# Layers 1 and 2 of a four-layer kernel: narrow products with exchanged operands, and the two token halves woven together

## The reference

```python
# layer 1: attention with the context as keys and values, then low-rank experts
a = jnp.einsum('bqd,bkd->bqk', query, key); c = softmax(a) @ key
q = x @ Wq_w.T; scores = q @ keys.T                  # 64 experts
top_vals, top_idx = jax.lax.top_k(scores, 16); gate = one_hot(top_idx) * softmax(top_vals), summed
z = x @ A_w.T                                        # 64 experts x rank 8
out = (z * gate) @ B_w.T * 2
# layer 2: attention, then three dense experts (tanh, gelu, silu), two of them chosen by sequence
Q = text @ Wq.T + bq; K = features @ Wk.T + bk; attended = softmax(Q @ K.T / sqrt(512)) @ features
gate_logits = concat([h, modality_ratio]) @ gate_w + gate_b
```

## Time and profile before

| what | before |
|---|---|
| median of 3 runs | 1708.53 us (1702.16 to 1709.68) |
| the profiled execution, its time | 1711.2 us |
| its span, first to last instruction | 1709.4 us |
| mean granted clock of TensorE | 0.893 |
| PE busy | 1443.9 us (84%) |
| PEld busy | 1131.2 us (66%) |
| DVE busy | 1083.9 us (63%) |
| ACT, POOL busy | 458.6 us (27%), 296.5 us (17%) |
| DMA, mean over the span | 56 GB/s |

### The profile page before, as it was taken

How to read it: one execution, slowest core, us unless ns; L and a number is a source line. 1 busy time by engine, 2 the same in 40 slices (tenths; PEclk the granted TensorE clock), 3 DMA queues, 4 the chain that set the end, 5 groups by cost and what they waited for, 6 DMA issues and landing times.

```text
span 1709.4 us, 18898 instructions
## 1 busy us (share of the span) xinstructions
PE 1443.9 (84%) x6489; PEld 1131.2 (66%) x6489; DVE 1083.9 (63%) x2489; ACT 458.6 (27%) x994; POOL 296.5 (17%) x170
## 2 busy tenths in 40 slices
PE   6569999998999898899646878858999778789998
PEld 5347776776677667688545767747887546567786
DVE  4556876767777666948886756554446399944142
ACT  3223423332343333313131202101221333322010
POOL 4101111111111111202021002111543121012120
PEclk9779999999999999999855699557999889899999
DMA  5521232322232212222001112200112000001011
GB/s 184 159 77 46 80 82 68 82 74 58 64 89 71 75 50 69 72 66 67 25 26 46 42 40 60 63 18 1 50 49 62 26 25 1 1 27 60 16 36 49
DMA packets 99407, 96.40 MB, mean 56 GB/s; under 512 B 13138, under 2 KB 72418, under 8 KB 99314
## 3 DMA queue, kind: packets, MB, share of 16 engines
q1 hardware_dynamic: 98802, 94.35, 19.0%
q0 software_dynamic: 512, 0.85, 0.2%
HBM read 84.34 MB, written 10.82 MB: 56 GB/s over the span
## 4 chain that ended last, share of the span: by engine, by line
PE 62%; DVE 25%; issue 4%; ACT 4%; DMA 2%; SPq 1%; POOL 1%; DVEq 0%; ACTq 0%; POOLq 0%
PE bank L1636 48%; PE bank L1977 5%; PE bank L1728 4%; DVE nf_y L1581 3%; DVE st L1141 2%; DVE xn L1159 1%; PE bank L1661 1%; DVE xT L1118 1%; PE bank L1718 1%; DVE mx L1192 1%; DVE mx L1498 1%; ACT e L936 1%; DMA nf_w<-in_L_w 1%; DVE sm L1510 1%; SPq L767 1%
## 5 line engine op out<-in xcount | busy, mean ns | idle before, releaser
L1636 PE MATMUL bank<-xT,slots 128*128 128x512 f32 (+1 forms) x1920 | 467.6, 402 | 9.6 <-DVE xT L1118 7.8
L1636 PEld LDWEIGHTS bank<-xT,slots 128*128 128x128 f32 (+1 forms) x1920 | 354.8, 186 | 109.0 <-issue 8.9
L813 POOL TENSOR_TENSOR slots<-staging,slots 128x1024 fp32r<-128x1024 f32 (+4 forms) x97 | 230.5, 2379 | 1103.0 <-ACT slots L903 1103.0
L1581 DVE TENSOR_SCALAR nf_y<-nf_w 128x512 fp32r<-128x512 f32 (+2 forms) x495 | 232.2, 496 | 29.0 <-PE bank L1977 28.0
L1636 PE MATMUL bank<-slots,h 128*128 128x512 f32 (+1 forms) x728 | 178.8, 405 | 20.1 <-DVE h L1248 13.9
L1977 PE MATMUL bank<-nf_y,nf_d 128*128 128x512 f32 (+2 forms) x495 | 170.6, 429 | 10.3 <-DVE nf_y L1581 8.0
L1636 PEld LDWEIGHTS bank<-slots,h 128*128 128x128 f32 (+1 forms) x728 | 140.8, 194 | 56.1 <-DVE h L1248 14.8
L903 ACT ACTIVATE slots<-staging 128x1024 fp32r<-128x1024 f32 (+4 forms) x97 | 98.1, 1018 | 189.9 <-PE bank L1636 174.2
L936 ACT ACTIVATE e<-bank,mx 128x320 f32<-128x320 f32 x128 | 66.4, 523 | 271.1 <-DVE mx L1195 254.0
L1977 PEld LDWEIGHTS bank<-nf_y,nf_d 128*128 128x128 f32 (+1 forms) x495 | 95.3, 197 | 47.0 <-issue 15.5
L1214 DVE TENSOR_TENSOR x<-bank,x 128x512 f32<-128x512 f32 x72 | 49.7, 690 | 110.9 <-PE bank L1636 110.6
(11 more groups left out here) (246 smaller groups left out, 1897.8 us busy)
## 6 DMA issues: line engine op xcount, KB each, us to landing
staging<-in_L_wqkT SPq DMA_DIRECT2D x16, 480.0 KB, 3.8
nf_out<-nf_w SPq DMA_DIRECT2D x30, 256.0 KB, 2.1
staging<-nf_out SPq DMA_DIRECT2D x30, 256.0 KB, 2.8
staging<-in_L_woT SPq DMA_DIRECT2D x16, 384.0 KB, 3.5
staging<-in_L_w SPq DMA_DIRECT2D x12, 512.0 KB, 4.0
nf_a<-nf_max SPq DMA_DIRECT2D x40, 128.0 KB, 3.6
nf_r<-nf_rcp SPq DMA_DIRECT2D x40, 128.0 KB, 3.4
nf_w<-in_L_w SPq DMA_DIRECT2D x15, 256.0 KB, 4.4
```

Of the source, the lines that this page charges most:

```text
L813: g.tensor_tensor(lo, split_source(i), hi.bitcast(FP32), ALU.subtract).then_inc(*sig.mark("weight_low", i))
L1581: v.tensor_scalar(nf_y[0:rows, i % STAIR_RING, 0:size], w_, bound, first, compare, ALU.mult)\
L1636: ins = mm(dst, l_, r_, start=i == 0, stop=i == len(passes) - 1)
```

## The change

*Operands exchanged.* `raw1(layer, b)` makes the scores transposed: 64 key columns are stationary and 256 token columns move, 12 passes a sequence. ScalarE copies them to `raw` (in layer 2 with the scale and, as a bias, `c2T`), and `scores1` is now two PE transposes back to 128 tokens by 64. `raw_route1(half)` and `raw_gate2(half)` do the same with 64 and 4 stationary columns and 512 moving ones, ScalarE copies to `rawT`, and four transposes a half bring them back. Routing then runs on four tiles at once (`route1(half)`, `gates1(half)`). The probabilities stay unscaled; the scale goes into the add to `x`. `pv1` is parted into `probs1` (transposes, splits) and `pv1`. `c2` has 4 stationary columns in place of 128 and is transposed by `c2t`.

*Halves woven.* `schedule` puts `k2` and `m2` between the products of attention 1, routing and `z1(0)` of half 0 before the end of half 1's attention, `stats(3,1)` before the first `zt1`, and the scores of half 0 of layer 2 before the last `b1`. The background ends before `raw_gate2(0)`. Weight chunks `k2` and `m2` are loaded before `z1` and `b1`; the gate weights, `wq1` and `keyT` are loaded in layer 0, where `router1` runs as well. `h2` is parted into four tensors, one of them above the background's memory.

```diff
-BACKGROUND_END = "gate2"
+BACKGROUND_END = "raw_gate2"
@@ schedule @@
-    steps += [("down0", 0, t) for t in range(TILES)]
+    steps += [("down0", 0, t) for t in range(TILES)] + [("router1",)]
...
+    steps += [("k2", 0), ("raw1", 1, 0), ("raw1", 1, 1), ("k2", 1), ("scores1", 1, 0), ("bias2",), ("k2", 2),
+              ("scores1", 1, 1), ("turn", 2, 1), ("probs1", 1, 0), ("k2", 3), ("raw1", 1, 2), ("pv1", 1, 0),
+              ("probs1", 1, 1), ("raw1", 1, 3), ("c2",), ("scores1", 1, 2), ("pv1", 1, 1), ("stats", 3, 0),
+              ("m2", 0), ("probs1", 1, 2), ("scores1", 1, 3), ("m2", 1), ("pv1", 1, 2), ("m2", 2), ("turn", 3, 0),
+              ("raw_route1", 0), ("probs1", 1, 3), ("z1", 0), ("c2t",), ("route1", 0), ("pv1", 1, 3), ("m2", 3),
+              ("gates1", 0), ("stats", 3, 1)]
...
+    after = {0: [("turn", 3, 1), ("raw_route1", 1)], 1: [("route1", 1)], 2: [("gates1", 1)],
+             4: [("stats", 4, 0)], 6: [("turn", 4, 0), ("raw1", 2, 0), ("raw1", 2, 1)],
+             7: [("scores1", 2, 0), ("scores1", 2, 1)]}
     for t in range(TILES):
+        steps += [("z1", t + 1)] * (t not in (0, 6, 7)) + [("zt1", t)] + [("b1", t - 1)] * (t > 0) + after.get(t, [])
+        steps += [("z1", t + 1)] * (t in (0, 6))
+    steps += [("probs1", 2, 0), ("b1", TILES - 1), ("stats", 4, 1)]
...
+    steps += [("pv1", 2, 0), ("probs1", 2, 1), ("pv1", 2, 1), ("stats", 5, 0), ("turn", 4, 1), ("raw1", 2, 2), ("raw1", 2, 3),
+              ("scores1", 2, 2), ("scores1", 2, 3), ("turn", 5, 0), ("raw_gate2", 0), ("probs1", 2, 2), ("gate2", 0),
+              ("pv1", 2, 2), ("probs1", 2, 3), ("hid2", 0, 0, 0), ("pv1", 2, 3), ("stats", 5, 1)]
...
+    steps += [("hid2", 0, c, 0) for c in range(1, KT)] + [("turn", 5, 1), ("raw_gate2", 1), ("hid2", 0, 0, 1), ("gate2", 1)]
+    steps += [("moe", 0), ("hid2", 0, 1, 1), ("moe", 1), ("hid2", 0, 2, 1), ("moe", 2), ("hid2", 0, 3, 1), ("moe", 3)]
@@ WEIGHT @@
-"scores1": 2, "pv1": 1.6, "route1": 1, ... "gate2": 1.2
+"raw1": 1.2, "scores1": .8, "probs1": .4, "pv1": 1.2, "raw_route1": 3, "route1": 1, ... "raw_gate2": 3, "gate2": .4
@@ ScalarE @@
+            def raw1(layer, b):
+                act.wait_ge(*sig.when("raw1_product", (layer, b)))
...
+                    sc.activation(raw[:, b % 2], psum(("raw1", layer, b))[0:CTX, 0:S], ACT.Copy)\
+                        .then_inc(*sig.mark("raw1_kept", (layer, b)))
@@ DVE: cut @@
-                link(v.tensor_tensor(f[:, 4], f[:, 1], f[:, 3], ALU.subtract))
+                link(v.tensor_tensor(f[:, 1], f[:, 1], f[:, 3], ALU.subtract))
@@ DVE: pv1 @@
+                    add_to_x("pv1", (layer, b, i), TPB * b + i, psum(("pv1", layer, b, i))[:], scale=sm[:, b % 4, 2 + i:3 + i])
@@ DVE: route1 @@
+            def route1(hf):
+                dve.wait_ge(*sig.when("route1_product", hf))
+                link(v.tensor_copy(r1[:, 0], psum(("route1", hf))[:, 0:TPH * NE].rearrange("p (t n) -> p t n", t=TPH)))
+                tops = top8[:, :, hf * TPH:(hf + 1) * TPH]
+                for pick in range(2):
+                    for t in range(TPH):
+                        ins = v.max(tops[:, pick, t], r1[:, pick, t])
+                    link(ins)
+                    for t in range(TPH):
+                        ins = v.match_replace(r1[:, 1, t], tops[:, pick, t], r1[:, pick, t], -1e30)
+                    link(ins)
...
@@ PE @@
+            def raw1(layer, b):
...
+                pairs = [([keys[:, q, k, b * CTX:(b + 1) * CTX] for q in range(2)], xt(k, b * S, (b + 1) * S))
+                         for k in range(KT)]
+                product(bank[0:CTX, 0:S], pairs).then_inc(*sig.mark("raw1_product", (layer, b)))
+            def raw_route1(hf):
...
+                pairs = [([rw[:, q, k] for q in range(2)], xt(k, hf * HALF, (hf + 1) * HALF)) for k in range(KT)]
+                product(bank[0:NE], pairs).then_inc(*sig.mark("raw_route1_product", hf))
+            def raw_gate2(hf):
...
+                pairs = [([gw[:, q, k] for q in range(2)], xt(k, hf * HALF, (hf + 1) * HALF)) for k in range(KT)]
+                product(bank[0:4], pairs).then_inc(*sig.mark("raw_gate2_product", hf))
```

More of the change, by code:

```diff
@@ L243 @@
 WEIGHT = {"v0": 1.9, "k0": 2.6, "kc0": .7, "q0": 2.6, "scores0": .9, "turn0": .4, "pv0": 1, "o0": 2.6, "up0": 2.6,
-          "down0": 4.8, "scores1": 2, "pv1": 1.6, "route1": 1, "z1": 2.6, "zt1": .5, "b1": 2.6, "k2": 1.3, "m2": 1.3,
-          "gate2": 1.2, "hid2": 2.6, "out2": 2.6, "k3": 1.3, "v3": 1, "q3": 2.6, "scores3": 1.3, "turn3": .5,
+          "down0": 4.8, "raw1": 1.2, "scores1": .8, "probs1": .4, "pv1": 1.2, "raw_route1": 3, "route1": 1, "z1": 2.6, "zt1": .5, "b1": 2.6, "k2": 1.3, "m2": 1.3,
+          "raw_gate2": 3, "gate2": .4, "hid2": 2.6, "out2": 2.6, "k3": 1.3, "v3": 1, "q3": 2.6, "scores3": 1.3, "turn3": .5,
           "pv3": 1.3, "o3": 2.6, "up3": 2.6, "down3": 4}
@@ L389, in build @@
         s0.close()
+        routing = ExitStack()
+        wq1 = sb("wq1", [ROUT, D], FP32, routing)
+        keyT = sb("keyT", [ROUT, NE], FP32, routing)
+        rw = sb("rw", [P, 2, KT, NE], F32R, routing)
         l = ExitStack()
@@ L394, in build @@
         g0 = sb("g0", [P, 2, HALF], FP32, l)
-        f0 = sb("f0", [P, 2, 5, HALF], FP32, l)
+        f0 = sb("f0", [P, 2, 4, HALF], FP32, l)
         l.close()
@@ L445, in build @@
         ra = sb("ra", [P, 4, TILES], FP32, l)
+        sb("between", [P, 2330], FP32, l)
+        h2[0, 0] = sb("h2_0_0", [P, 2, KT, HALF], F32R, l)
+        hf2 = sb("hf2", [P, 2, HALF], FP32, l)
         l.close()
@@ L539, in build @@
         for i in range(2):
+            chunk(("k2", i), P, (2, D), [((slice(None),), by_k(a["L2_wkT"], 2 * i, 2 * i + 2))])
+        for i in range(2):
             chunk(("ctxN", i), CTX, (2, D),
@@ L1980, in _ @@
             handlers = {"nf_sum": nf_sum, "turn": turn, "v0": v0_, "k0": k0_, "kc0": kc0_, "q0": q0_, "scores0": scores0, "turn0": turn0,
-                        "pv0": pv0, "o0": o0, "down0": down0, "scores1": scores1, "pv1": pv1, "router1": router1,
-                        "route1": route1, "z1": z1, "zt1": zt1, "b1": b1, "c2": c2_, "gate2": gate2, "moe": moe,
+                        "pv0": pv0, "o0": o0, "down0": down0, "raw1": raw1, "scores1": scores1, "probs1": probs1, "pv1": pv1,
+                        "router1": router1, "raw_route1": raw_route1, "route1": route1, "z1": z1, "zt1": zt1, "b1": b1,
+                        "c2": c2_, "c2t": c2t, "raw_gate2": raw_gate2, "gate2": gate2, "moe": moe,
                         "hid2": hid2, "out2": out2, "v3": v3_, "q3": q3_, "scores3": scores3, "turn3": turn3,
```

301 lines of the change are left out of this document (143 added, 158 removed), and 4 rows, old and new, of the table LAYER_STAGES.

## The result

The changed kernel takes 1666.27 us (median of 4 runs, 1664.69 to 1667.94) beside 1708.66 for the kernel before on the same chip: ratio 0.9753, interval 0.9731 to 0.9775. That is 42.4 us less. The forecast was 1647, 61 less; its range (1617 to 1681) holds the result. Run again beside later experiments, the same kernel gave 0.9741 (0.9717 to 0.9765).

What follows compares the result with a forecast made beforehand. Neither PE nor DVE was thought full: the stretch was a string of hand-offs. Segment savings 0 + 25 - 22 + 27 + 31 = 61 us, off 1708.5, gave 1647; range 1617 to 1681.

Steps and rivals of the forecast that it cites:

- The walk: Segment by segment from 859.3 us to expert 1, the new order's DVE blocks and hand-offs added up: 61 us less.
- 79, 53 and 37: Forecast us to the first zg, from last b1 to x after attention 2, and on to expert 1; before 103.8, 80.3, 68.1.
- 215 against 132 to 206 ns: Exchanged products: cost of a PE pass with 64 moving columns against one with 256, upper to lower clock.
- A price by moving columns alone: Rival on the exchanged products: passes cost by moving columns only, so PE gets 21 us more work; 1676, chance 0.03.
- Edits at nothing: Moved router1, weight loads and background jobs cost nothing; at worst 1 us uncovered, or 2.5 for a late slot's split.
- 859.3 to 881.8: stays: From layer 0's feed-forward end on PE to xT of the first half: unchanged at 22.5 us.
- To the end of b1: z/b stretch, first zg to last b1: 65.8 becomes 88 us, with half 1's routing on DVE mostly beside PE (1.5).
- the old wait of 6.48: In the z/b stretch, PE's wait for zg of tile 5 during DVE's next-layer statistics, forecast to stay.
- The operand exchange: Scores, routing and gate logits with fewer, wider passes: PE relieved of 37 us, about half on the path.
- the 27 and 31 of its last two segments: Us forecast saved between last b1 and x after attention 2 (27), and from there to expert 1 (31).
- the first rival: PE's clock stays at its upper level, 0.92, over the stretch of the change: 20 us more saved, 1627; chance 0.13.
- The second rival (1677): The weave gives only half: four of six DVE statistics blocks each expose 7.4 us more, 30 lost; chance 0.14.

Runs made afterwards that it cites:

- e1_bill: The changed kernel with 3.2 added to the background planner's room total, giving 612.6 as in the kernel before: 1663.31 us, ratio 0.972 to the kernel before.
- e7_route_out: The changed kernel without the maxima and replacements of half 1's routing on VectorE (results not the reference's): 1662.2 us, ratio 0.9724 to the kernel before.
- e8_turn41: e1_bill with attention 2's half-1 transposes and raw1 of batches 2 and 3 moved ahead of stats(5,0): 1654.44 us, ratio 0.9681 to the kernel before.
- e9_lead: e8_turn41 with long VectorE blocks in the z/b stretch placed after the next tile's gating and z1 two tiles ahead: 1646.4 us, ratio 0.9632.

## Why the prediction came out as it did

**Right**: faster, inside the range. The walk held where it added up DVE's blocks: 79, 53 and 37 against 78.7, 51.5 and 36.6, a pause of 14.2 before the first `zt1` (12 forecast), 508.7 behind the choice. In the first of these, two errors cancel: DVE was busy 64.5 us where 61 were counted, and the rest was 14 where 18 were. 215 against 132 to 206 ns held too, a little short at its upper end: the new groups took 1.6 to 2.8 us a sequence, up to 235 ns a pass. A price by moving columns alone, by which the exchange would have cost PE 20 us, is excluded: it saved 44 in passes alone. The prediction took that price from the Trainium skill ("TensorE: Matmul & The Clock Gate", Back-to-back issue gap) without its condition. The page gives it for a matmul by itself and says that in a stream with weight loads it comes out too low at few columns; the trace agrees, with 215 ns for 64 columns where the price gives 53.

**Wrong, step "Edits at nothing" with "859.3 to 881.8: stays".** The bill of 609.4 against 612.6 was noted and then dropped. It moved an item of the background to a place where its loads and DVE's chain were late. The first profile shows 9.1 us; `e1_bill` puts the edit's share at about 4. The same step had the new order of the weight loads at "one split, 2.5 us" if a slot came late. What came with it is another thing: splits that now fall beside DVE's chain in layer 0, and a wait there that is longer by 3.

**Wrong, step "To the end of b1", routing of half 1 on DVE, "mostly beside PE (1.5)".** It is exposed in full, 3.4 by `e7_route_out`. The step kept the old wait of 6.48 (6.96 here) and had no room for the new ones of 3.08 and 3.63, for `z1(1)` (2.9) and for 11 more background passes on PE (2.3). And an nf job was priced at 0.5: line L1604 in two stretches of the changed kernel,

```profile
890.90:969.60 78.70, 18.30 (x27) 0.83 0.25 71
...
969.60:1069.40 99.80, 17.48 (x43) 0.86 0.11 35
```

gives 0.68 us each in the first (11.56 for 24 in the earlier trace rows), so 5 us more for DVE there. DVE came to 197.6 us from the end of layer 0 to expert 1, not 188.

**Wrong, step "The operand exchange", "about half of it on the path".** In the order of before 40 of 44 us were, since DVE waited for these passes, and the other products got the upper clock besides. So the exchange as a whole gave 44 of the stretch, 4 of them on DVE. The walk's 61 would then leave 17 for the weave, which gave 8: the 27 and 31 of its last two segments were nearly right, the price in the z/b stretch was not. One walk for both parts hid how much hung on which, and that the sum is off by no more than 19 is in part luck: it had the exchange too small and the weave too large.

**The rivals.** The clock rose over the stretch, from 0.69 to 0.83, near the bound set for the first rival, but the 20 us that it hung on this did not come on top: the segments were as long as forecast, with DVE's blocks as their length. The second rival (1677) names what happened, blocks of statistics and routing exposed, but in one stretch and at 12 us, not 30. The measured 1666 lies nearer to it than to the forecast of 1647.

## What to carry to other kernels

When two dependent chains are interleaved, look first at the stretch that receives the work: where the engine is already nearly full, each moved microsecond is paid there, and the gain must come from the waits it leaves elsewhere. Order an in-order engine by what the other engine needs next: a short operation that releases work goes ahead of a long block that nobody waits for yet (`e8_turn41`, `e9_lead`: 0.009 of the time together, for no change in work). Test a compound change as a square of its parts: here one part carried it, and the sign of the other hung on the first. And a background placed by a total bill moves everywhere when the bill moves, so hold the bill fixed when comparing orders.

## What the runs showed of the hardware

**Narrow passes.** In the kernel before, a pass of 64 moving columns costs about as much as one of 256 at either clock: 12 took 1.50 us at the upper (125 ns) and 2.60 at the lower (217 ns), beside 132 and 206 ns for 256. So the exchange saves by the number of passes, 144 in place of 384 in the groups above. And while such passes ran, with one background pass between the dozens, the granted clock was 0.50 although PE was busy all the time; it was at 0.81 and 0.87 in the 10 us in which transposes and a product of 512 columns ran between them, and fell back to 0.50 in the next 64-column passes (columns as in the earlier trace rows, the clock behind POOL):

```profile
955.00:960.00 5.00, 5.00 (x22) 4.72 (x23) 3.32 (x18) 1.17 (x4) 0.85 (x1) 0.50 0.56 171
960.00:965.00 5.00, 5.00 (x27) 4.51 (x26) 4.07 (x17) 2.53 (x6) 0.00 (x0) 0.81 0.18 50
965.00:970.00 5.00, 4.35 (x30) 3.85 (x28) 4.14 (x12) 0.63 (x1) 0.00 (x0) 0.87 0.16 44
970.00:975.00 5.00, 5.00 (x24) 4.90 (x24) 3.75 (x21) 0.70 (x3) 0.00 (x0) 0.50 0.01 3
```

```profile
953.43 2.60 PE L1636 MATMUL bank<-rw,xT 128*128 128x64 f32 x12
...
966.45 1.50 PE L1636 MATMUL bank<-rw,xT 128*128 128x64 f32 x12 [0.65 <-issue]
```

**DVE beside POOL.** A DVE pass that takes 0.42 us took 1.4 to 2.5 where it overlapped a split on POOL. DVE and POOL in the changed kernel:

```profile
1056.23 0.56 DVE L1614 SCALAR_TENSOR_TENSOR nf_w<-bank,nf_a 128x384 f32<-128x384 f32 x1 [0.29 <-PE bank L2027]
1056.70 2.46 DVE L1604 TENSOR_SCALAR nf_y<-nf_w 96x512 fp32r<-96x512 f32 x1
1059.08 0.68 DVE L1375 TENSOR_TENSOR zg<-bank,gates 128x512 f32<-128x512 f32 x1
...
1074.12 2.03 DVE L1174 TENSOR_SCALAR rt<-mv 128x4 f32<-128x4 f32 x1
```

```profile
1056.54 2.34 POOL L817 TENSOR_TENSOR slots<-staging,slots 128x1024 fp32r<-128x1024 f32 x1 [71.48 <-ACT slots L909]
...
1073.79 2.34 POOL L817 TENSOR_TENSOR slots<-staging,slots 128x1024 fp32r<-128x1024 f32 x1 [0.26 <-ACT slots L909]
```

In both, DVE's instruction ends within 0.3 us of POOL's, and even one over 4 columns takes 2 us: it is held, not slowed in proportion. This is the 3.63 us wait for `zg` above. Seven DVE instructions between 890.9 and 1157.5 took 1.4 to 2.5 us in this way, three in the kernel before. The Trainium skill, "SBUF — State Buffer", Who interferes with whom, states such a lock between DVE and GpSimd, held for a whole instruction; the trace agrees. No run here took the splits away; the nearest is the pass for `h` above, 2.45 us beside a split and 0.42 where none ran.
